# Four-bit feed-forward: input coding and pass in one block that hands its PSUM banks on, with the code difference on VectorE and the excess on ScalarE

## The reference

```python
def fp4_quant_dequant(x):          # blocks of 16 along the last dimension
    xb = x.reshape(shape[:-1] + (shape[-1] // 16, 16))
    scale = jnp.maximum(jnp.max(jnp.abs(xb), axis=-1, keepdims=True) / 6.0, 1e-12)
    idx = jnp.searchsorted(_MID, jnp.abs(xb / scale))
    return (_GRID[idx] * jnp.sign(xb) * scale).reshape(shape)   # grid 0, .5, 1, 1.5, 2, 3, 4, 6
gate, y = fp4_linear(x, w_gate), fp4_linear(x, w_up)            # 128 -> 352, both operands coded
return fp4_linear(jax.nn.silu(gate) * y, w_down)                # 352 -> 128
...
x = x + _L0_ffn_ref(_layernorm(x, axis=-1), w_gate, w_up, w_down)
```

## Time and profile before

| | us |
|---|---|
| median of 3 runs | 2164.16 (2164.16 to 2165.03) |
| the profiled execution | 2161.56 |
| its span | 2159.8 |
| mean granted TensorE clock | 0.941 of full |

### The profile page before, as it was taken

How to read it: one execution, slowest core, us unless ns; L and a number is a source line. 1 busy time by engine, 2 the same in 40 slices (tenths; PEclk the granted TensorE clock), 3 DMA queues, 4 the chain that set the end, 5 groups by cost and what they waited for, 6 DMA issues and landing times. The chain is left out here.

```text
span 2159.8 us, 36543 instructions
## 1 busy us (share of the span) xinstructions
PE 1836.5 (85%) x12003; PEld 886.7 (41%) x12003; DVE 1680.9 (78%) x2274; ACT 1400.2 (65%) x2314; POOL 1056.2 (49%) x1121
## 2 busy tenths in 40 slices
PE   5558886687886857999999999999999967789997
PEld 2123332553664423555555555555554423222222
DVE  5979996596346958888888888888887636798884
ACT  3547774375335736777777777777776524689994
POOL 0167774364106714666666666666666521431112
PEclk9779998699997979999999999999999978999999
DMA  3000000000000011111111112221111100422210
GB/s 96 0 15 0 0 0 0 1 1 1 0 0 0 1 57 42 48 62 62 58 62 59 56 61 62 62 62 61 57 56 64 42 20 15 103 75 58 57 48 39
DMA packets 71432, 84.48 MB, mean 39 GB/s; under 512 B 20544, under 2 KB 44032, under 8 KB 71168
## 3 DMA queue, kind: packets, MB, share of 16 engines
q1 hardware_dynamic: 69536, 81.69, 12.5%
q10 hardware_dynamic: 1728, 0.67, 0.1%
HBM read 71.95 MB, written 9.57 MB: 38 GB/s over the span
## 5 line engine op out<-in xcount | busy, mean ns | idle before, releaser
L1761 DVE SCALAR_TENSOR_TENSOR fu_kv<-fu_ps_kv,fa_vec,fu_kv 128x511 f32<-128x511 f32 (+2 forms) x384 | 286.0, 746 | 56.3 <-ACT fu_kv L1633 51.1
L1844 POOL TENSOR_TENSOR fu_ds<-fu_p 128x768 f32<-128x768 f32 x64 | 115.8, 1810 | 188.7 <-PE fu_ps_ss L1532 188.5
L2199 ACT ACTIVATE rt_p<-rt_ps_s 128x1024 f32<-128x1024 f32 x192 | 185.6, 1029 | 25.1 <-PE rt_ps_s L2130 25.1
L1492 PE MATMUL fu_ps_s<-fu_qn,fu_kn 64*128 64x512 f32 (+3 forms) x1024 | 190.0, 468 | 1.4 <-DVE fu_sg L1722 0.7
L625 POOL TENSOR_TENSOR scan_hC<-scan_h,scan_c 128x1024 f32<-128x1024 f32 x64 | 150.9, 2357 | 71.7 <-DVE scan_h L601 71.7
L1633 ACT ACTIVATE fu_kv<-fu_ps_kv,fa_vec 128x512 f32<-128x512 f32 x128 | 88.4, 690 | 108.2 <-PE fu_ps_kv L1541 64.9
L1522 PE MATMUL fu_ps_n<-fu_p,fu_vt 128*64 128x512 f32 (+3 forms) x1024 | 151.9, 439 | 0.0
L601 DVE TENSOR_TENSOR_SCAN scan_h<-scan_dA,scan_ps_b 128x1024 f32<-128x1024 f32 x64 | 146.4, 2287 | 2.2
L524 PE MATMUL scan_ps_y<-scan_hC,w_ident 128*128 128x512 f32 x256 | 125.5, 612 | 26.5 <-POOL scan_hC L625 14.9
L2095 POOL TENSOR_SCALAR rt_d<-rt_d 128x1024 f32<-128x1024 f32 x32 | 35.0, 1094 | 184.0 <-DVE rt_d L2220 178.3
L1860 POOL TENSOR_TENSOR fu_kn<-fu_ks,fu_rb 128x512 f32<-128x512 f32 x64 | 81.5, 1274 | 68.8 <-DMA fu_rb<-rms_rows 68.7
(11 more groups left out here) (384 smaller groups left out, 5316.7 us busy)
## 6 DMA issues: line engine op xcount, KB each, us to landing
fu_rb<-rms_rows SPq DMA_DIRECT2D x256, 128.0 KB, 2.9
fu_ro<-rms_rows SPq DMA_DIRECT2D x128, 128.0 KB, 3.0
ra_stackq<-rope_parts SPq DMA_DIRECT2D x168, 32.0 KB
ra_stackk<-rope_parts SPq DMA_DIRECT2D x168, 32.0 KB
w_X<-in_xT SPq DMA_DIRECT2D x4, 512.0 KB, 7.3
fa_wp<-in_wp SPq DMA_DIRECT2D x8, 256.0 KB
fa_cr<-ncum_rows SPq DMA_DIRECT2D x128, 3.0 KB
rope_parts<-ra_hi SPq DMA_DIRECT2D x16, 128.0 KB, 2.5
```

What stands on the lines that cost most here:

```text
L1492: pe.matmul(sps[:, h, at:at + T - t * P], k[head(h), t * P:(t + 1) * P], q[head(h), t * P:T], start=(at == 0), stop=False)
L1761: dve.scalar_tensor_tensor(acc, kvps[:, at, 0:T - j], vec[:, a % GA, w:w + 1], acc, ALU.mult, ALU.add).then_inc(done, 1)
L1844: pool.tensor_tensor(DS[:, :, :], P0[p % 2][:, :, P:T], P13[:, :, 0:3 * P], ALU.add).then_inc(s.d1, 1)
L2199: act.activation(p[:, :, :], sps[unit(g, t, i) % RING][:, :, :], ACT.Exp, scale=DH_B ** -0.5).then_inc(s.exp, 1)
```

## The change

The two blocks become one block `ff`, with two sets of semaphores, c for the coding and s for the pass. The PSUM of the pass is that of the coding: gates use the third pair of banks, ups the first, `turn` the second, and `down` the two banks of `qps`. For each there is a wait on the coding operation that was the last to use the bank (c.q, c.out). In PE's order gates(0) and ups_of(0) stand ahead of back(2), and gates(1) ahead of back(3). In ACT's order gated(0) stands ahead of out(2), and out(3) behind the work on the first pair. The block scales are made for batches 0 and 1, then, behind the scaling of these two, for batches 2 and 3.

The coding itself is done in other steps. ACT makes Abs and then Relu of Abs minus 1.5 * 2^22, the excess `over`. DVE adds 1.5 * 2^22 and the scaled value to it, in PSUM (`code_total`), and then forms `over` + 1.5 * 2^22 - total (`minus_code`), which is the code with its sign turned. POOL only multiplies by the block's scale, in two halves. The sign is turned back in ACT's copy to `XQ` (scale -1). The table set for the silu is loaded behind the Exp of the statistics. The statistics are as before, under other names, and so is the rest of the pass.

```diff
-        with Stage(nc, "fx") as st:
+        with Stage(nc, "ff") as st:
+            BATCHES = B // 2
...
-            size, mag, tot, q, xq = ([st.sb(f"{n}{k}", [P, NB, FQ]) for k in range(2)] for n in ("size", "mag", "tot", "q", "xq"))
...
-        with Stage(nc, "fh") as st:
+            c_size, c_over, c_q, c_xq = ([st.sb(f"{n}{k}", [P, NB, FQ]) for k in range(2)] for n in ("csize", "cover", "cq", "cxq"))
+            c = st.sems("cent sq lnv rough var v1 v2 rstd amax normed above inv both xn size over tot q xq back out", "c_")
             PAIRS, LAG = NT * B // 2, 2
-            gps = st.ps("g", [P, 2, T])
-            ups = st.ps("u", [P, 2, T])
-            tps = [st.ps(f"t{k}", [P, KF, P]) for k in range(2)]
-            yps = [st.ps(f"y{k}", [P, T]) for k in range(2)]
+            gps = cps[2][:, :, :].rearrange("p (e a) q -> p e (a q)", e=2)
+            ups = cps[0][:, :, :].rearrange("p (e a) q -> p e (a q)", e=2)
+            tps = [cps[1][:, k * NB // 2:k * NB // 2 + KF * XB, :].rearrange("p (c a) q -> p c (a q)", c=KF) for k in range(2)]
+            yps = qps
...
+                    def center(g):
+                        k, before = g % BATCHES, g - RING
+                        if before >= BATCHES:
+                            pe.wait_ge(c.q, before - BATCHES + 1)
+                        elif before >= 0:
+                            pe.wait_ge(c.sq, TOK * (before + 1))
+                            pe.wait_ge(c.amax, before + 1)
...
+                    def back(k):
+                        for j in range(2):
+                            pe.wait_ge(c.xq, 2 * k + j + 1)
+                            pe.wait_ge(c.out, max(2 * k + j - 1, 0))
+                            for t in range(NT):
+                                a = (j * NT + t) * XB
+                                m = pe.transpose(qps[j][:, t * P:(t + 1) * P], c_xq[k % 2][:, a:a + XB, :].rearrange("p a q -> p (a q)"), w.ident[:, :])
+                            m.then_inc(c.back, 1)
...
                     def gates(k):
+                        pe.wait_ge(c.out, 2 * k // NT + 1)
                         pe.wait_ge(s.gt, k)
...
                     def turn(j):
+                        if j < 2:
+                            pe.wait_ge(c.q, BATCHES)
...
                     def down(m):
+                        if m < 2:
+                            pe.wait_ge(c.out, B)
...
+                    for g in range(BATCHES + RING):
+                        center(g)
+                    center(BATCHES + RING)
+                    back(0)
+                    back(1)
+                    pe.wait_ge(c.q, 2)
                     gates(0)
+                    pe.wait_ge(c.q, 3)
                     ups_of(0)
+                    back(2)
                     gates(1)
+                    back(3)
                     for k in range(PAIRS + LAG + 1):
...
+                    def sizes(k):
+                        act.wait_ge(c.xn, k + 1)
+                        act.wait_ge(c.over, max(k - 1, 0))
+                        act.activation(c_size[k % 2][:, :, :], cps[(BATCHES + k) % RING][:, :, :], ACT.Abs, scale=STEP).then_inc(c.size, 1)
+                        act.wait_ge(c.size, k + 1)
+                        act.wait_ge(c.q, max(k - 1, 0))
+                        act.activation(c_over[k % 2][:, :, :], c_size[k % 2][:, :, :], ACT.Relu, bias=w.below_round).then_inc(c.over, 1)
+                    def out(k):
+                        for j in range(2):
+                            act.wait_ge(c.back, 2 * k + j + 1)
+                            act.activation(XQ[:, 2 * k + j, :], qps[j][:, :], ACT.Copy, scale=-1.0).then_inc(c.out, 1)
...
+                    act.activation(rough[:, :, :], lnv[:, :, :], ACT.Exp, scale=-0.5).then_inc(c.rough, 1)
+                    act.preload_act_table_set("silu_and_others")
...
+                    sizes(0)
+                    sizes(1)
+                    sizes(2)
+                    out(0)
+                    sizes(3)
+                    out(1)
                     gated(0)
+                    out(2)
                     for k in range(PAIRS + LAG):
...
                         if real(k):
                             limited(k)
+                        if k == 0:
+                            out(3)
...
+                    def codes(half):
+                        pairs = slice(half * BATCHES // 2, (half + 1) * BATCHES // 2)
+                        r = widen(rstd[:, pairs, :].rearrange("p k t -> p (k t)"), XB)
+                        dve.wait_ge(c.rstd, 1)
+                        dve.wait_ge(c.amax, BATCHES)
+                        dve.tensor_tensor(per_token(normed, pairs), per_token(c_amax, pairs), r, ALU.mult).then_inc(c.normed, 1)
...
+                    def code_scaled(k):
+                        xn = cps[(BATCHES + k) % RING][:, :, :]
+                        dve.wait_ge(c.both, 2 * k // BATCHES + 1)
+                        dve.wait_ge(c.cent, BATCHES + k + 1)
+                        dve.tensor_tensor(xn, xn, widen(both[:, k, :], FQ), ALU.mult).then_inc(c.xn, 1)
+                    def code_total(k):
+                        xn = cps[(BATCHES + k) % RING][:, :, :]
+                        dve.wait_ge(c.over, k + 1)
+                        dve.scalar_tensor_tensor(xn, c_over[k % 2][:, :, :], ROUND, xn, ALU.add, ALU.add).then_inc(c.tot, 1)
+                    def minus_code(k):
+                        dve.wait_ge(c.tot, k + 1)
+                        dve.wait_ge(c.xq, max(2 * k - 2, 0))
+                        dve.scalar_tensor_tensor(c_q[k % 2][:, :, :], c_over[k % 2][:, :, :], ROUND, cps[(BATCHES + k) % RING][:, :, :], ALU.add, ALU.subtract).then_inc(c.q, 1)
+                    for k in range(BATCHES):
+                        block_maxima(k)
+                    roots()
+                    codes(0)
+                    code_scaled(0)
+                    code_scaled(1)
+                    codes(1)
+                    for k in range(BATCHES):
+                        code_total(k)
+                        if k + 2 < BATCHES:
+                            code_scaled(k + 2)
+                        minus_code(k)
...
+                    HALF = NB // 2
+                    for k in range(BATCHES):
+                        pool.wait_ge(c.q, k + 1)
+                        pool.wait_ge(c.above, 2 * k // BATCHES + 1)
+                        for j in range(2):
+                            pool.wait_ge(c.back, max(2 * k + j - 3, 0))
+                            blocks = slice(j * HALF, (j + 1) * HALF)
+                            pool.tensor_tensor(c_xq[k % 2][:, blocks, :], c_q[k % 2][:, blocks, :], widen(c_above[:, k, blocks], FQ), ALU.mult).then_inc(c.xq, 1)
```

More of the change, by code:

```diff
@@ L710, in ffn0_stages @@
             squares = [st.sb(f"sqr{k}", [P, P]) for k in range(2)]
-            ssq, var, lnv, rough, v1, v2, rstd = (st.sb(n, [P, PAIRS, TOK]) for n in ("ssq", "var", "lnv", "rough", "v1", "v2", "rstd"))
-            amax, normed, above, inv, both = (st.sb(n, [P, PAIRS, NB]) for n in ("amax", "normed", "above", "inv", "both"))
-            size, mag, tot, q, xq = ([st.sb(f"{n}{k}", [P, NB, FQ]) for k in range(2)] for n in ("size", "mag", "tot", "q", "xq"))
-            s = st.sems("cent sq lnv rough var v1 v2 rstd amax normed above inv both xn size mag tot q xq back out")
@@ L873, in _ @@
                 def _(pe):
+                    def center(g):
[5 more added lines that the diff above has]
+                            pe.wait_ge(c.amax, before + 1)
+                        for t in range(TOK):
+                            n, at = 2 * k + t // NT, t % NT * P
+                            m = pe.matmul(cps[g % RING][:, t * XB:(t + 1) * XB, :].rearrange("p a q -> p (a q)"), X[:, n, at:at + P], w.center[:, :], start=True, stop=True)
+                        m.then_inc(c.cent, 1)
+                    def back(k):
[6 more added lines that the diff above has]
+                            m.then_inc(c.back, 1)
                     def tokens(j):
@@ L921, in _, with moments @@
                 def _(act):
+                    act.preload_act_table_set("natural_log_exp_and_others")
+                    def moments(k):
+                        act.wait_ge(c.cent, k + 1)
+                        for t in range(TOK):
+                            act.wait_ge(c.sq, max(TOK * k + t - 1, 0))
+                            tile = cps[k % RING][:, t * XB:(t + 1) * XB, :].rearrange("p a q -> p (a q)")
+                            act.activation(squares[t % 2][:, :], tile, ACT.Square, accum_out=ssq[:, k, t:t + 1]).then_inc(c.sq, 1)
+                    def sizes(k):
[10 more added lines that the diff above has]
+                    for k in range(BATCHES):
+                        moments(k)
+                    act.wait_ge(c.sq, TOK * BATCHES)
+                    act.activation(lnv[:, :, :], ssq[:, :, :], ACT.Ln, bias=w.eps_ln[:, 0:1], scale=1.0 / D).then_inc(c.lnv, 1)
+                    act.wait_ge(c.lnv, 1)
```

(10 more changed lines are left out.)

152 lines of the change are left out of this document (27 added, 125 removed).

## The result

The changed kernel takes 2141.36 us, median of 4 runs (2139.95 to 2145.37), the kernel before beside it 2164.16 (4 runs, 2162.28 to 2165.03): ratio 0.9909, 95% interval 0.9887 to 0.9931. Forecast were 2146.2 us, in a range of 2138 to 2157. The profiled execution, at 2145.37 the longest of the four, has a span of 2143.5 us. The traced execution of the kernel before has 2159.8.

A forecast was written before the change was run, and what follows sets the result against it. DVE's list bounds the pass, POOL's coding the stretch before, so the second product's start sets each call's end. Gains of 9.2 and 8.8 us sum to 18.0: span 2141.8, run 2143.6, median 2146.2 us, range 2138 to 2157.

The forecast's parts named there:

- Rivals 4 and 5: In the pass: DVE operations meeting POOL cost 9 us per call (2164); PE at low clock loses 4.6 (2173); chance 0.03 each.
- block scales: On DVE before coding: made in halves of 128 columns, 1.90 us each instead of 3.03, so scaling starts 1.13 us earlier.
- Relu: New ACT operation in each coding batch, between 0.88 and 1.28 us, taken as 1.15.
- code_total and minus_code: Two new wide DVE operations per coding batch, taken as 1.22 us each, the next start after 1.14.
- POOL's half: Each half of POOL's scale multiplication in a coding batch, between 1.05 and 2.10 us, taken as 1.06.
- DVE's wait for the center call: In coding, scale(3) needs center(7), which waits for minus_code(0) to free its bank: DVE idles 2.6 us.
- Rival 3: In coding: new DVE operations cost 2.35 us each, product(1) at 428.9, gain 4.9 per call, 2154.4 us; chance 0.08.
- PE's clock at the hand-over: PE becomes fast about 5 us after gates(0) starts at 415.05, at 420.3; product(1) between 424.6 and 425.4.
- The walk: Call 1 step by step: back(2) until 421.2, gates(1) 1.4, back(3) 1.2, ups_of(1) 1.4, then product(1).
- rival 1: At the hand-over: PE fast by 415, product(1) at 422.8, gain 11 us per call, 2142 us; chance 0.12.
- Rival 2: At the hand-over: PE slow over back(2), gates(1), back(3), ups_of(1); product(1) at 428.6, gain 5.2 per call, 2153.8 us; chance 0.12.
- the signs named ahead: First product 21 to 22 us, second 25.5 to 26.5 behind first scaling; DVE waits 3 to 4 and about 1 us.

The follow-up runs named there:

- e1: Changed kernel with the hand-over order undone on PE and ACT (all four backs before the first gates), still one block and new coding: 2151.75 us, ratio to before 0.9948.
- e2: Changed kernel with the old coding arithmetic (DVE maximum and sum, POOL difference, no Relu), hand-over and single block kept: 2151.56 us, ratio to before 0.9956.
- e8: Kernel before, still two blocks, with the new coding and the block scales in halves: 2146.80 us, ratio to before 0.9931.
- e5: Changed kernel with minus_code(k) ahead of scale(k + 2) on DVE: 2134.46 us in one run, 2135.07 when timed again, ratio to before 0.9875.
- t1: Kernel before with every transpose of back issued twice on PE: 2161.29 us in one run.
- t2: Kernel before with the transposes of back made as plain matmuls with the identity: 2156.13 us in one run.

## Why the prediction was right, and where its sizes were off

**What bounds.** Right. The call's end follows the second product in all fourteen traces, and the pass keeps 10.1 us per two pairs. Rivals 4 and 5 (the pass gives it back, PE falls in the pass) are out: L985 and L990 cost 1.21 and 1.20 as before.

**The coding.** Each term stood within about 0.2 us: block scales 1.90 (measured 397.85 - 395.95 = 1.90), Relu 1.15 (1.149), code_total and minus_code 1.22 (1.224, 1.217), POOL's half 1.06 (1.057), DVE's wait for the center call 2.6 (2.81), minus_code(3) done 416.55 (416.46), POOL done 418.75 (418.61). Rival 3 (2.35 us per new operation) is out. gates(0) came at 414.54, 0.5 sooner than 415.05: the second half of back(1) started at 413.88 instead of 414.05, and gates(0) 0.66 behind it instead of 1.0.

**The hand-over.** It took place, and is worth 3.4 us per call (e1); the coding is worth 4 to 5 within one block (e2) and, with the halves of the block scales, 5 to 6 within two (e8). By steps from before, in calls 1 and 2: 5.0 and 6.2 for the coding in two blocks (e8), 3.4 and 2.1 more for one block with the old order (e1 against e8; this is more than the 0.9 of the block's change, and the table's load and the clock at gates(0) are in it), 3.5 and 3.3 more for the order of the hand-over. Together they are the 11.9 and 11.55 of M.

**The step that was mis-sized: PE's clock at the hand-over.** "PE had become fast about 5 us after 425.30; from 415.05 that is 420.3", with product(1) between 424.6 and 425.4. It rose near 417.5, 3 us after gates(0), and in call 2 1.7 after it. So back(2) took 1.04 and gates(1) 1.35 straight behind ups_of(0), and product(1) stood at 422.80. That is 1.8 under the forecast's 424.6: 0.5 at gates(0), 0.8 from there to the first product, 0.5 between the products. The walk itself adds up to 421.2 + 1.4 + 1.2 + 1.4 = 425.2, so the sum had already taken the lower end of its range; against the walk it is 2.4. That 422.80 is also the figure of rival 1 (422.8) is luck: rival 1 had the clock high by 415, and gates(0) still took 2.55 us. The gain of P1 is 38.73 - 27.74 = 10.99 in call 1 and 10.97 in call 2, not 9.2 and 8.8. A fixed delay behind the first matmuls was the wrong model: the rise came 5 us behind gates(0) in before, 3 in the changed kernel, inside it in e1, and ahead of it in e5. Rival 2 (slow over backs, gates and ups) did not happen in the changed kernel; the nearest to it is e2, where the clock fell again at ups_of(1). So two of the signs named ahead came out lower: the first product stood 20.8 us behind the first scaling and the second 24.95 (21 to 22 and 25.5 to 26.5 expected), after waits of 2.22 and 0.68 us (3 to 4 and about 1). The rest of call 1's 11.9 is its tail, where the last group of `down` but one took 4.84 instead of the earlier trace rows's 5.49:

```profile
498.86 4.84 PE L794 MATMUL ff_ps_q<-ff_ht,w_down 128*128 128x512 f32 x6 [2.11 <-ACT ff_ht L863]
```

**Between the calls.** The linear attention and call 2's statistics were put at nothing. From the last residual add of call 1 to the first roots operation of call 2 it was 120.8 us before and 119.0 after, 1.8 less. This isn't shown to come from the change: it was 119.4 in t1 and 119.3 in t2, which have the statistics and blocks of before, and 122.1 in e2. Together 11.9 + 11.55 + 1.8 = 25.2, where 18 were forecast.

**What no step held.** The 9 us behind call 2. The sum took everything behind the call as fixed. The two misses, +7.2 and -8.9, nearly cancelled in the profiled execution (2145.37 against the sum's 2143.6), which is luck and no merit of the sum; the median is lower because other executions were up to 5.4 us shorter than the profiled one. Whether these lost less behind call 2 isn't seen, as they have no trace.

## What to carry to other kernels

Find the wait that comes last in the stage and follow what feeds it: here the second product, 86 us ahead of the end, set the whole call. Where PE has gaps, price its work at both clock levels and don't derive from one trace when it will be fast. And compare two traces beyond the changed stage: a stage of unchanged instructions came out 5 to 9 us longer behind the changed one, with PE's clock in another position at its start and more of DVE's small operations slow beside POOL.

## What the runs showed of the hardware

- A DVE operation with one operand in SBUF and one in PSUM kept its 1.22 us for 1024 columns in the five of eight cases of call 1 that lay beside POOL's multiplications, while one with its input and output in SBUF (L824 of before) took 2.35 beside POOL and 0.69 where POOL was idle (call 2, at 648.16).
- A DVE operation of 128 x 8 elements took 0.2 us in most of its 64 times and 0.9 to 2.0 in 3 to 15 of them, each time beside an operation of POOL; but 48 to 60 of the short ones lay beside POOL as well.
- One block more per call, with nothing in it but a 0.06 us memset, made what follows each call start 2.7 to 3.1 us later than in the two traces of the changed kernel.
- The clock of TensorE rose under 128 x 128 float32 transposes alone in one call and not in the other (0.82, 0.57 over 14 us), and under as many matmuls the other way round (0.51, 0.88).
- With a pause in each call, behind which all starts about 6.2 us later, the granted clock 73 us behind the second one was 1.00 in the one trace, where it was 0.90 and 0.91 in the two of the changed kernel, and the stages behind were 6 us shorter.
